# Attention output made channel-major by transfers instead of TensorE transposes, in a two-layer conditioned transformer

## What is computed

```
for layer in (0, 1):                       # layer norm + gelu, then rms norm + swiglu
    h = norm(x) * (1 + scale) + shift
    q, k, v = rope(h @ w_q), rope(h @ w_k), h @ w_v
    o = softmax(q k^T / 4) v               # 16 heads, 512 x 512 scores each
    x = x + (o @ w_proj + b_proj) [* gate]
    h = norm(x) * (1 + scale) + shift
    x = x + (act(h @ w_1 + b_1) @ w_2 + b_2) [* gate]
```

## Time and profile before

| | |
|---|---|
| median of 3 runs | 794.48 us (793.76 to 796.32) |
| the profiled execution | 798.87 us |
| its span, first to last instruction | 797.0 us |
| mean granted TensorE clock | 0.983 |
| HBM traffic over the span | 94 GB/s |

### The profile page before, as it was taken

One profiled execution on the slowest core, in us unless ns is written; L12 is line 12 of the kernel. 1 busy time (PEld: TensorE's weight loads), 2 busy tenths in 40 slices (PEclk: granted clock), 3 DMA queues, 4 the chain that ended last, 5 costly groups with the idle time before them and its releaser, 6 DMA issues.

```text
span 797.0 us, 13586 instructions
## 1 busy us (share of the span) xinstructions
PE 753.3 (95%) x4800; PEld 467.1 (59%) x4800; DVE 627.0 (79%) x1097; ACT 478.3 (60%) x761; POOL 291.4 (37%) x267
## 2 busy tenths in 40 slices
PE   5979999999999999999999999999999999999697
PEld 3643334466545754565546664667646684668397
DVE  3878997798878988888788899968868878865454
ACT  1217764687658765786658876665466655565332
POOL 0502114443354535452464336232343232422343
PEclk9969999999999999999999999999999999999899
DMA  8569570433142411351141433541133411100000
GB/s 320 157 178 297 137 213 14 146 116 73 40 137 90 108 41 40 107 146 42 40 133 54 146 94 112 168 99 32 44 113 114 107 41 49 21 1 1 28 1 27
DMA packets 34163, 76.22 MB, mean 96 GB/s; under 512 B 4528, under 2 KB 9264, under 8 KB 33840
## 3 DMA queue, kind: packets, MB, share of 16 engines
q1 hardware_dynamic: 34096, 75.35, 33.3%
HBM read 39.42 MB, written 35.65 MB: 94 GB/s over the span
## 4 chain that ended last, share of the span: by engine, by line
PE 75%; DVE 7%; DMA 6%; issue 4%; POOL 3%; ACT 3%; SPq 2%; ACTq 0%; DVEq 0%; POOLq 0%
PE ring L1037 18%; PE ps_o L967 13%; PE ps_b L1054 12%; PE ring L937 9%; PE ring L952 8%; PE ring L901 5%; DVE top L1233 3%; PE ring L1007 3%; DMA kt<-scratch 3%; PE ring L914 2%; POOL sines L1603 2%; PE ring L978 2%; ACT pr L1489 1%; PE ring L883 1%; DMA qt<-top_t 1%
## 5 line engine op out<-in xcount | busy, mean ns | idle before, releaser
L1233 DVE TENSOR_REDUCE top<-ring 128x2 f32<-128x1024 f32 x256 | 307.4, 1221 | 53.5 <-PE ring L952 51.2
L1489 ACT ACTIVATE pr<-ring 128x1024 f32<-128x1024 f32 x256 | 255.9, 1024 | 84.0 <-PE ring L937 77.2
L1646 POOL TENSOR_TENSOR act_l<-mlp,act_h 128x256 fp32r<-128x256 f32 x128 | 102.8, 803 | 240.1 <-DVE act_h L1315 240.1
L967 PE MATMUL ps_o<-pr,va 128*17 128x512 f32 x1024 | 133.2, 602 | 0.1
L952 PE MATMUL ring<-kt,qt 48*128 48x512 f32 x512 | 112.9, 458 | 10.0 <-DMA kt<-scratch 4.5
L937 PE MATMUL ring<-qt,kt 49*128 49x512 f32 x512 | 114.1, 466 | 6.3 <-DMA qt<-top_t 3.2
L1526 ACT ACTIVATE mlp<-ring,col 128x256 f32<-128x256 f32 x128 | 60.5, 473 | 83.9 <-PE ring L1037 70.2
L937 PEld LDWEIGHTS ring<-qt,kt 49*128 49x128 f32 x512 | 46.5, 184 | 86.9 <-issue 41.8
L1037 PE MATMUL ring<-hh,wl 128*128 128x256 f32 x384 | 84.1, 301 | 2.9 <-DVE hh L1290 0.9
L1301 DVE SCALAR_TENSOR_TENSOR mlp<-mlp 128x256 f32<-128x256 f32 x128 | 59.3, 463 | 34.1 <-ACT mlp L1533 23.8
L952 PEld LDWEIGHTS ring<-kt,qt 48*128 48x128 f32 x512 | 48.5, 189 | 63.0 <-issue 22.4
(11 more groups left out here) (89 smaller groups left out, 1025.1 us busy)
## 6 DMA issues: line engine op xcount, KB each, us to landing
scratch<-high SPq DMA_DIRECT2D x48, 512.0 KB, 5.1
qt<-scratch SPq DMA_DIRECT2D x64, 192.0 KB, 3.7
kt<-scratch SPq DMA_DIRECT2D x64, 192.0 KB, 4.6
scratch<-low SPq DMA_DIRECT2D x16, 512.0 KB, 5.6
mlp<-in_w_split SPq DMA_DIRECT2D x20, 256.0 KB, 3.3
xs<-in_x SPq DMA_DIRECT2D x4, 512.0 KB, 5.6
out_x<-xs SPq DMA_DIRECT2D x3, 512.0 KB, 2.9
pr<-in_w_ada SPq DMA_DIRECT2D x2, 512.0 KB, 7.6
```

The costliest lines, as they stand in the source:

```text
L967: last = nc.tensor.matmul(ps_o[32 * h:32 * h + HD + 1, :], va[:, u % 2, t, QUAD * g + h, :], pr[:, slot, :], start=(t == 0), stop=(t == T ...
L1233: nc.vector.tensor_reduce(top[:, n % 2, 0:4 * T].rearrange("p (e c) -> p e c", e=2)[:, :, c], pair[:, :, :], AX_X, ALU.max, negate=True).t ...
L1489: nc.scalar.activation(pr[:, at % NP:at % NP + 2, :], pair[:, :, :], ACT.Exp, scale=SCALE).then_inc(free, 1)
L1646: nc.gpsimd.tensor_tensor(act_l[:, at % 2, :], src, act_h[:, at % 2, :].bitcast(F32), ALU.subtract).then_inc(act_l_in, 1)
```

## The change

For units 0 to 6 both turns of the output go. For each quad, SP issues eight small transfers within SBUF after ScalarE's copy: four that spread a head's 512 denominators over 16 partitions of `den`, 32 on each, and four that move a head's 16 rows of 512 numerators to their place among the channels in `o_rows`, a view of the tile of `o` (`gather`). For each two quads (k = 0, 1): VectorE takes the reciprocal of 128x32 elements (`invert`), SP writes them to a new DRAM tensor `dens` (`inverse`), SP reads them back so that each row of 512 lands on the 16 partitions of its head, 256 KB in all (`spread`), and GpSimd multiplies 128x512 into `hf` (`share`). `project` waits for `share` instead of for ScalarE's copy. Unit 7 keeps the old way. New waits: ScalarE's copy of quad n waits until the transfers of all quads before it have landed; SP's `spread` waits for its `inverse` to land. The tile `top` has 48 columns instead of 128, so the weights of its transpose have 48 columns.

```diff
+NTOP = 48
@@ quad_pieces
+    if n // NQ < LAST:
+        return pieces + [(at["output"][0], "act", "output", n), (at["output"][1], "sp", "gather", n)]
     return pieces + [(tick, engine, "output", n) for tick, engine in zip(at["output"], ("act", "pe", "dve"))]
@@ post_pieces
-    pieces = [(at["o"][0], "pe", "o_turn", u), (at["o"][1], "act", "channels", u, 0),
-              (at["o"][2], "act", "channels", u, 1)]
+    if u < LAST:
+        pieces = [(tick, engine, name, u, k) for k in range(KC)
+                  for tick, (engine, name) in zip(at["o"][k], (("dve", "invert"), ("sp", "inverse"), ("sp", "spread"),
+                                                              ("pool", "share")))]
+    else:
...
-        top = sb("top", [P, 2, P])
+        top = sb("top", [P, 2, NTOP])
@@ sync
+                def gather(n):
+                    u, g = quad_of(n)
+                    k, at = g // 2, g % 2 * STACK
+                    sp.wait_ge(o_free, n + 1)
+                    if u:
+                        sp.wait_ge(share_in, KC * (u - 1) + k + 1)
+                    for h in range(QUAD):
+                        r = at + HD * h
+                        sp.dma_start(den[r:r + HD, k, :], ot[32 * h + HD:32 * h + HD + 1, :]).then_inc(moved, 16)
+                    for h in range(QUAD):
+                        r = at + HD * h
+                        sp.dma_start(o_rows[r:r + HD, k, :], ot[32 * h:32 * h + HD, :]).then_inc(moved, 16)
+                def inverse(u, k):
+                    sp.wait_ge(inv_in, KC * u + k + 1)
+                    sp.dma_start(dens[k].rearrange("(p n) -> p n", p=P), den[:, k, :]).then_inc(inv_out, 16)
+                def spread(u, k):
+                    sp.wait_ge(inv_out, 16 * (KC * u + k + 1))
+                    if u or k:
+                        sp.wait_ge(share_in, KC * u + k)
+                    sp.dma_start(rec[:, :], dens[k].rearrange("(h n) -> h n", n=L).unsqueeze(1).to_broadcast(
+                        [P // HD, HD, L])).then_inc(spread_in, 16)
@@ tensor, project
-                        pe.wait_ge(*emptied("o", u, KC - 1))
+                        if u == LAST:
+                            pe.wait_ge(*emptied("o", u, KC - 1))
+                        else:
+                            pe.wait_ge(share_in, KC * (u + 1))
@@ vector
+                def invert(u, k):
+                    ve.wait_ge(moved, 16 * 2 * QUAD * (NQ * u + 2 * k + 2))
+                    nc.vector.reciprocal(den[:, k, :], den[:, k, :]).then_inc(inv_in, 1)
@@ scalar, output
-                    if n:
+                    if n > NQ * LAST:
                         ac.wait_ge(*filled("output", n - 1))
+                    elif n:
+                        ac.wait_ge(moved, 16 * 2 * QUAD * n)
@@ gpsimd
+                def share(u, k):
+                    gp.wait_ge(spread_in, 16 * (KC * u + k + 1))
+                    gp.wait_ge(moved, 16 * 2 * QUAD * (NQ * u + 2 * k + 2))
+                    if k == 0 and u == 0:
+                        gp.wait_ge(*filled(*LAST_H1[1]))
+                    elif k == 0:
+                        gp.wait_ge(hh_in, KC * u)
+                        gp.wait_ge(hl_in, KC * u)
+                    nc.gpsimd.tensor_tensor(hf[:, k, :], o_rows[:, k, :], rec[:, :], ALU.mult).then_inc(share_in, 1)
```

More of the change, by code:

```diff
@@ L125, in first_pieces @@
     return pieces + [("pe", "net_2", part) for part in range(NET_PARTS)] + [("dve", "net_2")]
[L128 to L163, removed]
- -726,
[L165 to L185, removed]
- -785,
[L187 to L196, removed]
+FIRST_AT = (-1761,
+ -907,
+ -1690,
+ -2202,
+ -1970,
+ -1438,
+ -2391,
+ -1305,
+ -1384,
+ -2133,
+ -1641,
+ -1617,
+ -1800,
+ -1398,
+ -1507,
+ -1347,
+ -1207,
+ -1923,
+ -1155,
+ -1109,
+ -1722,
+ -793,
+ -622,
+ -1555,
+ -1141,
+ -1391,
+ -999,
+ -1323,
+ -887,
+ -1079,
+ -666,
+ -1427,
+ -1255,
+ -1179,
+ -726,
+ -988,
+ -930,
+ -792,
+ -678,
+ -785,
+ -308,
+ -584,
+ -1180,
+ -755,
+ -1138,
+ -908,
+ -662,
+ -885,
+ -822,
+ -570,
+ -741,
+ -496,
+ -504,
+ -658,
+ -496,
+ -477,
+ -1491,
+ -1145,
+ -788,
+ -992,
+ -1162,
+ -976,
+ -830,
+ -735,
+ -523,
+ -472,
+ -334,
+ -301,
+ -388)
 def top_pieces(n):
@@ L245 @@
[L245 to L290, removed]
-STORE_AT = 444
[L292 to L303, removed]
@@ new lines @@
+SPLIT_AT = ({'act': (-1111, -631, -257, -83, 7, 56, 82, 100, 232, 308, 447, 526),
+  'dve': (-213, -199, -83, 24, 56, 107, 138, 149, 405, 481, 528, 555),
+  'load': (-1184, -573, -452, -250, -131, -107, -46, 48, 115, 167, 370, 564)},
+ {'act': (25, 48, 50, 85, 99, 117, 123, 137),
+  'dve': (29, 42, 42, 101, 121, 124, 163, 164),
+  'load': (-52, -31, -12, 6, 69, 114, 135, 177)})
+STORE_AT = 444
+LOAD_AT = {'row': -1665,
+ 'trig': -1215,
+ 'ada1': -1131,
+ 'ada2': -1823,
+ 'grow': -990,
+ 't1': -1391,
+ 't2': -864,
+ 'x1': -767,
+ 'wf0': -190,
+ 'wf1': -53,
+ 'x2': -325,
+ 'x3': -323}
@@ L654, in build @@
         o = sb("o", [P, T, C])
+        o_rows = o[:, :, :].rearrange("p t c -> p (t c)").rearrange("p (k q) -> p k q", k=KC)
+        den = sb("den", [P, KC, L // HD])
+        rec = sb("rec", [P, L])
         stats = sb("stats", [P, T, 6])
@@ L719, in build @@
         o_free = sem("o_free")
+        moved, inv_in, inv_out, spread_in, share_in = (sem(name) for name in ("moved", "inv_in", "inv_out", "spread_in",
+                                                                              "share_in"))
         x_new, bias_in = sem("x_new"), sem("bias_in")
@@ L864, in store @@
                         sp.dma_start(out_v[j], xs[:, j]).then_inc(x_out, 16)
-                whole_program("sp", {"load": load, "load_w": load_w, "spill": spill, "fill": fill, "top": top_row,
+                whole_program("sp", {"load": load, "load_w": load_w, "spill": spill, "fill": fill, "gather": gather,
+                                     "inverse": inverse, "spread": spread, "top": top_row,
                                      "store": store})
```

334 lines of the change are left out of this document (187 added, 147 removed).

## The result

The changed kernel takes **822.92 us** (median of 4 runs, 819.35 to 825.28) against 795.4 us for the kernel before in runs beside it: a ratio of 1.036, 95% interval 1.033 to 1.039. The forecast was 780.5 us, 766 to 796, and gave "slower" 0.15. It was wrong in sign: 28 us lost where some 14 were to be won (798.9 to 784.9, or 794.5 to 780.5).

A forecast was written before the change was run, and what follows sets the result against it. TensorE was taken to bound the kernel, VectorE next. 798.9 - 25.7 (gain) + 8.7 (waits at `project`) + 3.0 (queues) = 784.9 us; the profiled execution being 4.4 above the median, 780.5, range 766 to 796.

The forecast's parts named there:

- Gain, 25.7 us: Time saved: 24.2 us of transposes and waits off TensorE, 1.0 for the readers, 0.5 for the narrower `top`.
- 1.0 us for the readers: Gain from less work on VectorE and ScalarE, which read TensorE's ring: 1.0 us, ends 0 and 10.
- The chain, 15.7 us: New path per unit end, from ScalarE's copy of the last quad to `share`'s end: 15.7 us, 11.8 to 20.8.
- Waits at `project`, 8.7 us: TensorE's waiting where the chain outlasts the work beside it: 3.3, 2.9, 1.0, 0, 0, 0, 1.5 us, units 0 to 6.
- is counted already: At ends of units 0 to 2 part of the `project` wait would show at the top row, adding nothing.
- Reciprocal, 0.9 us: Chain link on VectorE: the reciprocal, 0.25 us, and up to one `peaks` of 1.22 in front; 0.3 to 1.5.
- Queues passed, 3.0 us: Loss from added work on the queues of SP and GpSimd and the moved order: 3.0 us, ends -5 and 10.
- rival 3: Slower through serial transfers, waits at `share_in` or the top row; gain gone at a chain of 18.1 us; chance 0.15.
- 1.7 us per wait: Possible clock cost: after a TensorE wait the next 5 us run at a lower granted clock, 1.7 us each.
- Rival 2: TensorE's freed time fills with waits for VectorE and ScalarE; half the gain lost, 793.3 us, 788 to 797; chance 0.15.
- Rival 1: The new path is fully hidden, chain near its low end of 11.8 us: 768.8 us, 764 to 772; chance 0.18.
- signs named for "wrong": Path over 18 or under 13 us, idle at all unit ends, ring waits up 10, first 100 us off by over 5.

The follow-up runs named there:

- e4: The changed kernel's new order with the old turns, division and copies put back, 48-column `top` kept: 848.7 us, 1.069 of the kernel before.
- e15: The kernel before with only the `top` tile narrowed from 128 to 48 columns: 795.3 us against 795.7.
- e1: The changed kernel with five of SP's top rows put ahead of the gather that stood right before them: 833.0 us.
- e2: The changed kernel with a quad's four denominator transfers merged into one by a partition step of 32: 804.2 us.
- e5: e2 with the denominators issued first on a semaphore of their own, so `invert` waits for them alone: 805.1 us.
- e8: The kernel before, old order and path, plus eight transfers per quad on SP into unread spare tiles and the 48-column `top`: 864.7 us.
- e14: e8 with its four denominator transfers as one, so five issues per quad on SP: 839.5 us.
- e10: e5 with all five transfers of a quad issued by ScalarE behind its copy instead of by SP: 919.2 us.
- e12: e8 with its eight transfers per quad issued by ScalarE instead of by SP: 1003.6 us.
- e13: e5 without the inverses' trip through DRAM, so the output is not divided: 792.4 us, 0.994 of the kernel before.

## Why the prediction was wrong

**Gain, 25.7 us: right as far as it was measured.** Between the two profiled executions TensorE's work is 20 to 21 us less at full speed. At the same ticks (e4) its busy time is 22.1 us less, and the whole 25.8, though that is a net of several things. The 1.0 us for the readers was not measured by itself. The 0.5 us for `top` is nothing that can be measured (e15), within its range of 0 to 4.5.

**The chain, 15.7 us: right in length.** The seven unit ends took 18.4, 14.9, 14.4, 13.7, 16.8, 18.4 and 19.2 us from the start of the copy to the end of `share`, mean 16.5, inside 11.8 to 20.8. Its links: eight issues 4.95 us at most ends against 4.0 taken (each 0.59, where I had put 0.5 between the rows of 0.39 and 0.64; the row of the same kind, SBUF to SBUF, was the right one). `invert` starts 1.4 us after the end of the last issue at five ends, against 2.2 taken for the landing. From the start of `inverse` to that of `spread` 1.4 us at five ends and 2.9 and 3.5 at the last two, against 2.5. From `spread` to `share` 3.6 to 4.9 us, mean 4.2, against 3.8; `share` 1.28 against 1.7. Issues and `spread` were over what was taken, the others mostly under.

**Waits at `project`, 8.7 us: wrong place.** TensorE waited for `share` 3.1 us in all. At the ends of units 0 to 2, where 3.3, 2.9 and 1.0 us were expected, it waited 7.07, 1.39 and 2.21 us, and for the top row: 10.7 us where 7.2 were expected. The sentence that failed is that the top row's wait "is counted already". It was taken for a part of the same wait. It is a wait of its own, set by when SP is done with the gather (130.20 at the end of unit 0) and not by the chain. And the cover of the chain is VectorE's work in those very pieces: while TensorE stands before `scores`, VectorE gets no `peaks`, so the stretch beside the chain does not run down but moves back with it. This last part is argued; no run separates it.

**Reciprocal, 0.9 us: the wrong question.** I asked what stands in front of `invert` on VectorE (up to one `peaks`) and not what stands behind it. VectorE waited there 20.9 us in ten waits, with `peaks` unread behind it. The longest, 5.41 us, cost nothing of its own, since TensorE stood for the top row meanwhile. Where the top row is there, this wait does hold TensorE: in e1 it grew to 29.7 us, TensorE's `scores` waited 18.6 us for VectorE, and the time grew by 10. e2 took most of it away, but together with a part of SP's holding, and in e5 the last 4 us of it gave nothing that can be measured. How the 18.8 us of e2 divide between the two is open.

**Queues passed, 3.0 us: the step that turned the sign.** "A queue that mostly waits" was read as one with time to spare. SP waits 172.9 us for `top_t` alone, and what it issues then is wanted at once. In the changed kernel itself, three issues less per quad gave 18.8 us back (e2). In the old order a gather of eight issues per quad costs 71 us and one of five 44 (e8, e14), with SP's standing for the copy in both; the high end of my range for this term was 10. e10 to e12 show that it is no property of SP: the same issues on ScalarE cost 4.1 and 6.1 us per quad. The new order avoids much of it (the loss is 28 us, where 71 less the gain of 26 would be 45), and pays for that: e4 is 55 us over the kernel before. How many of these the order costs the new path itself is open, since the new path was not tried in the old order.

**The clock: in rival 3 alone, and belongs in the sum.** TensorE's removed work is 20 us or more, its busy time fell by 4.3: some 16 us more went into slower execution, by the granted clocks. The 1.7 us per wait are the size of the stretch of 135 to 140 behind the wait of unit 0, and of the one behind that of unit 2. Behind those of units 1 and 4 it was 4 to 5 us (the stretches of 220 to 230 and 490 to 505 us, at 0.50 to 0.59 for the most part, worked out in the same way). I had multiplied by none.

**The rivals.** Rival 3 had the right place (the top row right behind the gather) and the right trigger for the clock, but the wrong price and break-even: it hung on a chain over 18.1 us, and the chain is 16.5 in the mean (18.4, 18.4 and 19.2 at three of seven ends). Rival 2 (waits for VectorE and ScalarE in place of the gain) came in part: TensorE's waits for VectorE's `top` went from 6.0 to 17.7 us. Rival 1 (path hidden, 768.8) is out even without its trip: e13 is at 792.4. Of the signs named for "wrong", these came: TensorE's waits for the ring up by over 10 us, three chains over 18 us, and idle time where none was expected, at the ends of units 4 (3.18 us, for VectorE) and 5 (1.48, for `share`); only that of unit 3 has none over 1 us. The copies within the first 100 us came 4.7 and 4.4 us late, just under the 5 named, and the last of unit 0 5.2.

## What to carry to other kernels

Price a DMA not by its landing but by what its issue holds up: take the issue time of the nearest row, times the count, and ask for the instruction behind it in the same in-order queue how soon it is wanted; idle time of a queue that waits for late events is not spare time. Where an engine with a long list gets a new wait, look at what stands behind the wait rather than in front of it. Merging small transfers by a partition step can be worth more than shortening the chain they are in: here three issues less per quad gave 18.8 us, and leaving out two whole DRAM transfers per half unit 9.5 (12.7 behind the merging).

## What the hardware did that was not expected

An issue of a transfer within SBUF took 0.59 us on SP and 0.61 on ScalarE (medians), for 2 KB and for 32 KB; the one with a partition step of 32 that replaces four took 0.61 (0.60 to 1.24). It is no busy time on the page of either engine, yet ScalarE does nothing else in it. The Trainium skill ("Perfetto Trace Analysis", section "DMA Instruction — HWDGE (DVE, Sync)") says that the data's movement lies outside the issuing instruction's window; the trace agrees: 0.59 us of issue, and 1.8 to 2.0 us from its start to the landing. Right behind the issues of a spill, at 123.26, four of them took 4.37 us, the longest 1.81; the DMA engines moved 345 GB/s from 120 to 125 us. Whether the one comes from the other is not shown.
